# A graph network kernel: the second message layer in three sum passes with projections among them, and the degrees of its nodes summed in two places

## The reference

```python
def _priv_conv(h, src, dst, n, Wl, bl, Wr, scale):     # 128 -> 256, then 256 -> 128
    xn = _l2norm(h)
    agg = jax.ops.segment_sum(xn[src], dst, num_segments=n)   # with a loop edge for each node
    h_norm = jnp.linalg.norm(h, axis=-1, keepdims=True)
    out = _l2norm(agg) * h_norm * scale
    out = out @ Wl + bl + h @ Wr
    return _l2norm(out)
...
x = x + _L0_gnn_ref(h, ...)                            # two _priv_conv with a relu between them
h = jnp.maximum(_layernorm(x, axis=-1), 0.0)
...
def gcn_conv(x, W, b, src, dst, mask, n):
    h = x @ W
    deg = 1.0 + jax.ops.segment_sum(ew, dst, num_segments=n)
    dinv = jax.lax.rsqrt(deg)
    norm = dinv[src] * dinv[dst] * ew
    agg = jax.ops.segment_sum(h[src] * norm[:, None], dst, num_segments=n)
    agg = agg + h * (1.0 / deg)[:, None]
    return agg + b
```

## Time and profile before

| | us |
|---|---|
| median of 3 runs | 1125.64 (1122.07 to 1128.34) |
| the profiled execution, its own time | 1124.67 |
| its span on the core | 1122.5 |
| TensorE busy / VectorE busy / ScalarE busy | 936.8 / 572.8 / 396.0 |
| mean granted clock of TensorE | 0.918 |

### The profile page before, as it was taken

The page is one execution under the profiler, slowest core; times in us unless marked ns, Lnnn a source line. Parts: engine busy times, 40 slices in busy tenths (PEclk is TensorE's granted clock), DMA queues, the critical chain, the costliest instruction groups (busy, mean ns, idle before and its releaser), DMA issues.

```text
span 1122.5 us, 17876 instructions
## 1 busy us (share of the span) xinstructions
PE 936.8 (83%) x7347; PEld 608.7 (54%) x7347; DVE 572.8 (51%) x1630; ACT 396.0 (35%) x869; POOL 79.9 (7%) x102
## 2 busy tenths in 40 slices
PE   0346999998799999979999978988876785778997
PEld 0335666766555556965465545655535443454654
DVE  4799999986921011642120267545542654445222
ACT  1538999982661000372010031544104402220300
POOL 2100000000000000000000000741014100020000
PEclk9759999999899999859999999998988787889999
DMA  6430000007100000011000002774114200140002
GB/s 192 136 84 1 1 2 1 2 1 318 49 1 1 1 1 1 2 68 52 1 1 1 1 1 61 258 214 141 27 25 119 60 1 1 30 175 29 33 1 59
DMA packets 39794, 60.39 MB, mean 54 GB/s; under 512 B 3822, under 2 KB 30721, under 8 KB 39192
## 3 DMA queue, kind: packets, MB, share of 16 engines
q1 hardware_dynamic: 31202, 38.17, 10.3%
q0 software_dynamic: 4592, 17.86, 5.2%
q10 hardware_dynamic: 3910, 3.12, 1.1%
HBM read 33.08 MB, written 30.85 MB: 57 GB/s over the span
## 4 chain that ended last, share of the span: by engine, by line
PE 55%; DVE 32%; ACT 5%; DMA 4%; issue 3%; POOL 1%; ACTq 0%; DVEq 0%; POOLq 0%; SPq 0%
PE psum L2800 24%; PE psum L2260 12%; DVE region L1010 7%; DVE region L1003 6%; PE psum L2568 4%; PE psum L2165 2%; DVE region L1517 2%; PE psum L2762 2%; DMA half_table<-region 2%; PE psum L2344 1%; PE psum L2190 1%; DMA nodebuf<-in_x 1%; POOL region L778 1%; DVE region L1251 1%; PE psum L2782 1%
## 5 line engine op out<-in xcount | busy, mean ns | idle before, releaser
L2800 PE MATMUL psum<-adj,region 128*128 128x448 fp8e4 x1050 | 201.8, 353 | 0.0
L2800 PEld LDWEIGHTS psum<-adj,region 128*128 128x128 f16 x1050 | 102.5, 98 | 92.9
L2260 PE MATMUL psum<-adj,region 128*128 128x448 fp8e4 x700 | 135.5, 355 | 3.1 <-DVE region L1244 3.1
L2190 PE MATMUL psum<-region 128*128 128x200 bf16 (+2 forms) x1176 | 111.0, 229 | 20.6 <-DVE region L1010 20.5
L2190 PEld LDWEIGHTS psum<-region 128*128 128x128 bf16 x1176 | 93.2, 99 | 55.0 <-DVE region L1010 30.4
L2260 PEld LDWEIGHTS psum<-adj,region 128*128 128x128 f16 x700 | 68.7, 98 | 66.8 <-issue 5.2
L2800 PE MATMUL psum<-region 128*128 128x448 fp8e4 (+2 forms) x426 | 83.7, 359 | 13.6 <-DVE region L1710 13.5
L1862 ACT ACTIVATE adj<-psum 128x400 fp8e4<-128x400 f32 x196 | 86.7, 518 | 19.4 <-PE psum L2194 18.8
L1010 DVE TENSOR_TENSOR region<-iota_key,region 128x1200 bf16<-128x1200 bf16 x147 | 92.7, 703 | 0.0
L2165 PE MATMUL psum<-adj,region 128*128 128x448 fp8e4 x350 | 91.7, 355 | 0.0
L778 POOL DMA_INDIRECT region<-adj_table,node_of x33 | 31.2, 945 | 848.3 <-DVE node_of L1647 731.3
(11 more groups left out here) (348 smaller groups left out, 1209.0 us busy)
## 6 DMA issues: line engine op xcount, KB each, us to landing
adj_table<-adj SPq DMA_DIRECT2D x1, 10000.0 KB, 27.2
edge_table<-edges SPq DMA_DIRECT2D x1, 4656.0 KB
region<-dk_dram SPq DMA_DIRECT2D x2, 1568.0 KB, 8.3
adj_table<-region SPq DMA_DIRECT2D x1, 2704.0 KB, 8.9
half_table<-region SPq DMA_DIRECT2D x2, 832.0 KB, 7.1
node_table<-region SPq DMA_DIRECT2D x1, 1650.0 KB, 8.4
xs_dram<-nodebuf SPq DMA_DIRECT2D x1, 1600.0 KB, 6.1
nodebuf<-xs_dram SPq DMA_DIRECT2D x1, 1600.0 KB, 6.1
```

The source lines that it names most:

```text
L2190: pe.matmul(psum[:, q % BUILD_BANKS, i * KEYS + k0:i * KEYS + k1], hot_lo[:, r, c, j, :, i], hot_key[:, r, c, j, k0:k1, i], start=(n == 0) ...
L2260: last = pe.matmul(psum[:, b, 0:BLOCK], weight(t, k), adj[:, t * PAD + b * BLOCK:t * PAD + (b + 1) * BLOCK], start=(t == 0 and k == 0), st ...
L2800: last = pe.matmul(psum[:, b, 0:width], here[:, t, k, :], rows, start=(t == 0 and k == 0), stop=(t == n_src - 1 and k == 1))
```

## The change

The second layer's sums of m = 0 stay as they are. Those of m = 1 become three passes of 4, 2 and 1 blocks (AGG_PASSES). In the second pass TensorE makes seven projection groups and 14 norms between the products, in the third three groups and 6 norms, and behind it three groups and 5 norms. The copies out of PSUM of the second and third pass, and their squares, are ScalarE's. The rows are finished in three parts of 14, 6 and 5 tiles; the third one's add x, squares and scaled rows, and the transposes of groups 3 to 6, stand inside the first pass of the next convolution.

The degrees come from two places. Of the sources' tiles 0 to 9, one-column products in the first layer (250 products). Of tiles 10 to 24, VectorE adds the 128 lanes of `adj` (`sum_lanes`, 14 adds of 3136 columns into `lane_degrees`, f16, in `nodebuf`), and TensorE sums over the lanes (25 products) in the first pass, at tile 22. `early_degrees` (VectorE) and the degrees' transpose follow from there. Since `nodebuf` holds the lanes, x is loaded again only after the degrees. `packed_masks` is moved from `unet` to a place ahead of the adds.

```diff
@@ -514,11 +517,26 @@
...
-        EARLY = 4
-        LN_PARTS = ((0, 12), (12, TILES))
-        LN_LATE = 10
+        AGG_PASSES = ((0, 4), (4, 6), (6, BLOCKS))
+        LN_PARTS = ((0, 14), (14, 20), (20, TILES))
+        PROJECT_BANKS = (0, 1, 2, 3, 0, 1, 2, 3, 4, 5, 0, 1, 2)
+        PROJECT_FREED = (0, 0, 0, 0, 2, 4, 6, 8, 0, 0, 10, 12, 14)
+        PROJECT_AT = ({4: (0,), 6: (1,), 9: (2,), 11: (3,), 14: (4,), 16: (5,), 18: (6,)}, {9: (7,), 12: (8,), 15: (9,)})
+        NORMS_AT = (8, 18)
+        ROWS_FIRST = (2, 3, 1)
+        DEGREES_AT, TURN_DEGREES_AT = 22, 2
+        TURNED_FIRST = 3
+        TURN_BANKS_2 = (4, 5, 3, 7, 4, 5, 6)
+        TURNED_BEFORE = (1, 2, 3, 4, 5, 6, 7)
...
         ROW_PARTS = ((0, 8), (8, TILES))
         TURN_LAG = 8
+        COLUMN_TILES = 10
+        EARLY_COLUMNS = 13
+        EARLY_COL = 32
@@ -643,7 +661,6 @@
...
-            load_x(sp, x_again)
@@ -660,14 +677,15 @@
...
-                sp.wait_ge(centered, 3)
+                sp.wait_ge(deg_ready, 1)
+                load_x(sp, x_again)
+                sp.wait_ge(dkrows_ready, 1)
+                sp.dma_start(dk_dram[0], dk_rows_early).then_inc(dk_out, DMA)
+                sp.wait_ge(centered, 1 + len(LN_PARTS))
                 sp.dma_start(xs_dram[0], nodebuf[:]).then_inc(xs_out, DMA)
-                sp.wait_ge(dkrows_ready, 1)
...
-                sp.wait_ge(blocks_out, BLOCKS * FIRST_UNIT)
+                sp.wait_ge(squared, len(LN_PARTS))
                 sp.dma_start(d_all, row[0:1, 0:COLS].broadcast_to((P, COLS))).then_inc(db_in, DMA)
@@ -1140,14 +1159,41 @@
...
+            def sum_lanes():
+
+                lanes = lane_degrees[:, 0:COLS]
+                for t in range(COLUMN_TILES + 1, TILES):
+                    of = adj[:, COLUMN_TILES * PAD:COLUMN_TILES * PAD + COLS] if t == COLUMN_TILES + 1 else lanes
+                    step(nc.vector.tensor_tensor(lanes, of, adj[:, t * PAD:t * PAD + COLS], ALU.add))
+                nc.vector.memset(lane_degrees[:, COLS:PAD], 0.0).then_inc(lanes_summed, 1)
+
+            def early_degrees():
+
+                d, kept, deg = dcol[:, 0, 0, :], dcol[:, 0, 1, :], tiny[:, 10, :]
+                dve.wait_ge(deg_ready, 1)
+                step(nc.vector.tensor_copy(deg, psum[:, 7, EARLY_COL:EARLY_COL + TILES]))
+                step(nc.vector.tensor_tensor(deg, deg, psum[:, 7, 0:TILES], ALU.add))
+                step(nc.vector.tensor_scalar(deg, deg, 1.0 / COUNT, 1.0, ALU.mult, ALU.max))
+                rsqrt(d, deg, tiny[:, 11, :])
+                nc.vector.tensor_tensor(d, d, kept, ALU.mult).then_inc(dk_ready, 1)
+
             def second_layer(norm1):
...
+                blocks_of(1, 0, 4, first_agg(agg1t[:, 0, :]))
+                blocks_of(1, 4, BLOCKS, first_agg(agg1t[:, 0, :]))
+                early_degrees()
+
+                def take_blocks():
+
+                    dve.wait_ge(agg_half, 4 + 1)
+                    for b in range(*AGG_PASSES[0]):
+                        first_agg(agg1t[:, 1, :])(b).then_inc(blocks_out, 1)
+
...
                 dve.wait_ge(x_again, 2 * DMA)
+                take_blocks()
+                add_squares(0)
+                dve.wait_ge(dk_turned, 1)
+                v.tensor_copy(dk_rows_early, psum[0:2 * TILES, 7, P:2 * P]).then_inc(dkrows_ready, 1)
+                combine_part(0)
                 add_x(0)
-                combine(LN_PARTS[1][0] // 2, LN_LATE)
+                add_squares(1)
                 scale_rows(0)
-                combine(LN_LATE, len(GROUPS2))
+                combine_part(1)
+                add_squares(2)
                 add_x(1)
+                combine_part(2)
                 scale_rows(1)
+                return add_x, scale_rows
@@ -1302,16 +1383,15 @@
...
                     norm1 = first_layer()
+                    packed_masks()
+                    sum_lanes()
 
...
-                    second_layer(norm1)
-                    degrees(0, by_edges)
-                    dve.wait_ge(h2t_ready, len(GROUPS4))
-                    return
+                    return second_layer(norm1)
@@ -1705,6 +1778,10 @@
...
+                        if i == 0 and t == 4:
+                            add_x(2)
+                        if i == 0 and t == 8:
+                            scale_rows(2)
@@ -1956,26 +2032,39 @@
...
+                def take_blocks(n):
+
+                    act.wait_ge(agg_half, 4 + n + 1)
+                    for b in range(*AGG_PASSES[n]):
+                        act.wait_ge(squares_added, b - 2)
+                        nc.scalar.activation(new_squares[:, b % 3, :], psum[:, b, 0:BLOCK], ACT.Square, scale=1.0 / (UNIT_SCALE * COUNT)).then_inc(sq_ready, 1)
+                        nc.scalar.activation(agg1t[:, 1, b * BLOCK:(b + 1) * BLOCK], psum[:, b, 0:BLOCK], ACT.Copy,
+                                             scale=1.0 / (UNIT_SCALE * COUNT)).then_inc(blocks_out, 1)
...
+                def keep_turned(g):
+
+                    t0, n = GROUPS4[g]
+                    act.wait_ge(h2_turned, g + 1)
+                    nc.scalar.activation(nodes_t[:, t0 * P:(t0 + n) * P], psum[:, TURN_BANKS_2[g], 0:n * P], ACT.Copy).then_inc(h2t_ready, 1)
+
+                block_squares()
                 unit_squares(0)
+                take_blocks(1)
                 center_squares(0)
+                second_rows(0)
+                take_blocks(2)
                 unit_squares(1)
-                second_rows(0)
+                keep_turned(0)
                 center_squares(1)
+                keep_turned(1)
+                keep_turned(2)
                 second_rows(1)
-                for g, (t0, n) in enumerate(GROUPS4):
-                    act.wait_ge(h2_turned, g + 1)
-                    nc.scalar.activation(nodes_t[:, t0 * P:(t0 + n) * P], psum[:, g % 4, 0:n * P], ACT.Copy).then_inc(h2t_ready, 1)
@@ -2060,6 +2158,15 @@
...
+                        if i == 0 and t == 4:
+                            unit_squares(2)
+                        if i == 0 and t == 8:
+                            keep_turned(3)
+                            center_squares(2)
+                        if i == 0 and t == 12:
+                            second_rows(2)
+                        if i == 0 and t % 4 == 0 and t >= 16:
+                            keep_turned(t // 4)
@@ -2345,24 +2445,56 @@
...
-                pe.wait_ge(blocks_out, 2 * BLOCKS + 4)
-                for g in range(EARLY):
+                def part_norms(n):
+
+                    t0, t1 = LN_PARTS[n]
+                    pe.wait_ge(squares_added, AGG_PASSES[n][1])
+                    pe.wait_ge(dkrows_ready, 1)
+                    for t in range(t0, t1):
+                        last = pe.matmul(psum[:, NORMS_BANK[n], NORMS_COL + t:NORMS_COL + t + 1], agg_squares[:, t * P:(t + 1) * P], ones[:, 0:1],
+                                         start=True, stop=True)
+                    last.then_inc(norm_ready, 1)
+
+                def sum_degrees():
+
+                    pe.wait_ge(lanes_summed, 1)
+                    for t in range(TILES):
+                        last = pe.matmul(psum[:, 7, t:t + 1], lane_degrees[:, t * P:(t + 1) * P], ones_col[:], start=True, stop=True)
+                    last.then_inc(deg_ready, 1)
+
+                for n, (b0, b1) in enumerate(AGG_PASSES):
+                    pe.wait_ge(blocks_out, BLOCKS + (4 if n == 0 else BLOCKS))
+                    for t in range(TILES):
+                        if n == 0 and t == DEGREES_AT:
+                            sum_degrees()
+                        if n == 1 and t == TURN_DEGREES_AT:
+                            turn_degrees(0)
+                        if n > 0 and t == NORMS_AT[n - 1]:
+                            part_norms(n - 1)
+                        for g in PROJECT_AT[n - 1].get(t, ()) if n > 0 else ():
+                            pe.wait_ge(blocks_out, 2 * BLOCKS + AGG_PASSES[n - 1][1])
+                            project_tiles(g)
+                        for k in range(2):
+                            for b in range(b0, b1):
+                                last = pe.matmul(psum[:, b, 0:BLOCK], parts1[:, t, k, P:2 * P], adj[:, t * PAD + b * BLOCK:t * PAD + (b + 1) * BLOCK],
+                                                 start=(t == 0 and k == 0), stop=(t == TILES - 1 and k == 1))
+                    last.then_inc(agg_half, 1)
+                pe.wait_ge(blocks_out, 3 * BLOCKS)
+                for g in range(LN_PARTS[2][0] // 2, len(GROUPS2)):
+                    if g == LN_PARTS[2][0] // 2 + 1:
+                        part_norms(2)
                     project_tiles(g)
-                pe.wait_ge(squares_added, BLOCKS)
...
-                degree_sums(0, False)
-                pe.wait_ge(proj_done, 2 * TILES)
...
-                turn_degrees(0)
+                pe.wait_ge(proj_done, TILES + LN_PARTS[1][1])
+                for g in range(TURNED_FIRST):
+                    turn_second(g)
+
@@ -2376,11 +2508,20 @@
...
```

(21 more changed lines are left out.)

159 lines of the change are left out of this document (82 added, 77 removed).

## The result

| | kernel before | changed kernel |
|---|---|---|
| median of 8 runs | 1122.57 us (1118.39 to 1128.34) | 1135.67 us (1128.37 to 1139.51) |
| profiled execution | 1124.67 us, span 1122.5 | 1135.8 us, span 1133.9 |
| ratio, with its 95% interval | | 1.0107 (1.0079 to 1.0135) |

The changed kernel is 1.1% slower: the forecast's side, and 2.7 us above its 1133. That distance flatters the forecast. It added 8.5 us to 1124.67, and the median of the kernel before, over eight runs, is 1122.57; the ratio makes the difference 12.0 us (8.9 to 15.2). In the profiled pair it is 11.4 us of span.

What follows compares the result with a forecast made beforehand. TensorE's sums, then ScalarE and VectorE's row work, were taken to bound 343 to 547 us. Next convolution 2.1 us later, plus 1.6, 1.2 and 3.6 inside it, made 8.5 on 1124.67: forecast 1133 us, range 1115 to 1139.

Steps and rivals of the forecast that it cites:

- Column products at nothing: First layer: 250 degree products moved there fit into TensorE's gaps to within 0.2 us each; cost taken as 0.
- Adds at 3.45 us, end 388.0: VectorE, ahead of the bank copies: fourteen adds at one element at a time, 48.3 us from 339.7.
- Stall 16.5: Before the first pass: TensorE waits 16.5 us, from 374.4 to 390.9, for bank copies behind the adds.
- Clock behind the stall 1.6: First pass: TensorE's clock falls in the stall, costing 1.6 us more.
- Clock in the second pass, 1.5 behind the 14 norms: TensorE's second pass: slow clock behind the 14 norms costs 1.5 us.
- x 8.5 us behind the degrees: Reload of x waits for the degrees at 426.6, lands at 435.1; first projection waits 3.0 us.
- The end of the seventh projection at 465.7: Second pass on TensorE: the seventh projection group ends at 465.7 us, and the row work starts from there.
- The row work of three parts: VectorE and ScalarE, from 465.7: three parts in place of two; next convolution's first sum product at 508.1, against 506.0 before.
- Inside the next convolution: Its first pass: transposes 1.6 us, group 3's copy wait 1.2, group 4's 3.6, with no gap there before.
- rival (c): TensorE's clock stays low: projections 3 us more, cold start of the next convolution 1.6, x load 1.5; 1139 us, 11%.
- Rival (b): Stall stays, rest shorter: x in 6 us (-2.5), clock holds behind norms (-1.5), group 4's copy in time (-3); 1127 us, 26%.
- Rival (a): VectorE's adds go two elements at a time, end at 365.3; the stall and its clock loss go; 1115 us, 17%.

Runs made afterwards that it cites:

- fifteen column tiles: Changed kernel with 15 source tiles counted by column products in place of 10, so nine VectorE adds in place of fourteen; ratio to the kernel before 0.9949.
- two-byte kernel: Changed kernel with thirteen of the fourteen adds reading f16 zeros in place of fp8 tiles; ratio to the kernel before 0.992 (one run).
- split kernel: Changed kernel with one add left in place, seven behind the copies of banks 0 to 3, six behind those of banks 4 to 6; ratio to before 0.9917.
- second trace: Trace of the changed kernel run again without any edit, in the second group; 1173.23 us, ratio to the kernel before 1.0111.
- first pair: The original runs of the kernel before and the changed kernel, chip not on record; 1122.57 and 1135.67 us, ratio 1.0107.
- second group: Follow-up kernels run on another chip than the first group, among them the unedited changed kernel: 1173.23 us, ratio to the kernel before 1.0111.
- few degrees: Kernel before with 25 of its 625 degree products, those of source tile 0 alone; ratio to the kernel before 1.0009.
- first group: Fifteen column tiles, split kernel, early degrees and two-byte adds, run on one chip; ratios to the kernel before 0.9949, 0.9917, 0.9878 and 0.992.
- early degrees: Split kernel with the 25 products that sum the degrees at tile 15 of the first pass in place of 22; ratio to the kernel before 0.9878.
- copy first: Early degrees kernel with ScalarE's copy of turned group 4 ahead of part three's rows in place of behind them; ratio to the kernel before 0.9852.

## Why the prediction was right, point by point

- Column products at nothing: right, to 0.2 us. Beyond 250 they cost some 28 ns each (3.5 us for 125), as the fifteen column tiles show.
- Adds at 3.45 us, end 388.0: 3.43 with 3.46 from start to start, end 388.5. Right, and the reason (one operand of one byte) is shown by the two-byte kernel.
- Stall 16.5: 16.6. That it passes on in full is shown by the split kernel.
- Clock behind the stall 1.6: 2.15, and 1.84 in the second trace. I took it from the 3.06 us gap, behind which 56 products lost 1.6 us.
- Clock in the second pass, 1.5 behind the 14 norms: mis-sized. From the first projection group (438.70) to the end of the seventh it took 29.5 us for 28.3 forecast, 3.4 of them slow clock: 1.7 behind the norms, near the forecast, and 1.8 at the first projection group and the products behind it, right after the wait for x, for which I had nothing.
- x 8.5 us behind the degrees: 9.0 (the degrees' products end 427.4, VectorE goes on 436.4). The first projection waited 3.55 for 3.0.
- The end of the seventh projection at 465.7: 468.2, the sum of the points above. The error went through to the next convolution (508.1 forecast, 510.1 measured).
- The row work of three parts: 42.4 forecast, 41.8 measured. Its sum is right, its path is not quite: I led the middle of it over VectorE's factors and combining. In the trace it goes over ScalarE, by part one's 14 rows (485.59 to 491.1), the copy of block 6 behind them and part two's squares, to 493.7, and VectorE waits 1.1 us for these. By the prediction's numbers the two ways are level (both have part two's x added at 495.4), so this cost nothing here.
- Inside the next convolution I had 6.4 us more than before; measured 5.8 (9.9 - 4.1). That this is close is luck, since its parts were off: group 3's wait of 1.2 never came, group 4's was 2.1 for 3.6, and the transposes took 1.0 for 1.6, since those of group 3 stood ahead of the first sum product. In their place came a cold start of 2.5 us, which stood only in rival (c): 3.17 us for eight sum products that took 1.69 before (505.98), 1.91 for a group of 1.05, and 0.2 behind it.
- The end of the pass before was set at 546.9. It is 549.9 (537.83 + 12.08 in the fence above), so all my absolute times for that pass are 3 us low. The sum used differences and was not touched.
- Rival (b)'s 1127 adds its 1.5 us to the median, where the forecast and the other two rivals add theirs to the profiled execution; by that it is 1126.

Forecast 8.5, measured 9.9 by the mark, 11.4 by the span and 12.0 by the ratio. By the mark the errors are +2.0 up to the next convolution (2.5 of slow clock, less 0.6 in the row work) and -0.6 inside it. So the mechanism held (adds ahead of the copies, stall, three row parts), and the term most in error was TensorE's clock: 3.1 us in the sum, 5.6 in the two passes and 2.5 in the next convolution. Rival (a) fell by the adds. Rival (b) had two of its three terms wrong (x took 9.0 us, the clock did fall) and the third partly right (group 4's wait). Rival (c)'s cold start and projections at half speed were both seen, but for shorter stretches than it said. What stays open is the 1.5 us behind the mark.

## What to carry to other kernels

Work that an idle engine takes over is free only at a place where nobody's release stands behind it: list what the engine would have done next and who waits for that, and cut long work around it. Here thirteen of fourteen adds, placed behind the two sets of copies in place of ahead of them, turned 1.1% slower into 0.8% faster. Before work is moved off an engine, leave it out of the kernel once: if the time stays, as with the degrees, it lay beside something else. And a chain can be shortened only by the slack of what runs beside it: with about 1 us of it, a step moved forward by 3.8 us gave 0.9. Last, before a gain is credited to an edit, take the pieces that ran at another clock out of it.

## What the runs showed of the hardware

**An fp8 source.** A VectorE add of 3136 columns to f16 takes 3.42 us with one or two fp8 sources and 1.79 with f16 ones.

**The same kernel in two places.** The changed kernel took 1135.7 us in the first pair and 1173.2 in the second group, and the traces differ by 2.2 us at the mark. The other 35 us arise while the adjacency rows are gathered: the last cast of them stands at 887.8 us and at 927.1. Of them, 23.7 (27.7 + 9.1 - 13.1) are at the start of it, at VectorE's first casts of the gathered rows, here in the first pair and then in the second group:

```profile
723.82 16.42 DVE L1597 CAST region<-psum 128x512 fp8e4<-128x512 f32 x28 [13.09 <-PE psum L2776]
```

```profile
742.29 0.69 DVE L1597 CAST region<-psum 128x512 fp8e4<-128x512 f32 x1 [27.68 <-remote]
752.11 3.79 DVE L1597 CAST region<-psum 128x512 fp8e4<-128x512 f32 x6 [9.13 <-remote]
```

In the first pair they wait 13.1 us, in the second group 27.7 and then 9.1. The GpSimd instructions that start these gathers take 0.94 us each in both. It is not this kernel's doing: the kernel before waits 13.4 us there in the first pair, the one with few degrees 30.3 and 6.4 in the second group, and the split kernel 25.3 and 11.2 on the chip of the first group. The traces don't say why; the median from issue to landing of the gathers at L797 is 4.1 us in the first pair and 7.5 in the changed kernel's second trace, but 4.2 in the split kernel, which waits as long.

**The clock behind one-column products.** The group that stands behind the 14 norms, 28 instructions of one column, takes 1.95 us at full clock. With the same instructions in the same order ahead of it, it took 3.00 and 3.62 us in the two traces of the changed kernel, 3.11 with fifteen column tiles, 3.37 with the early degrees and 3.19 with the copy first, but 1.95 in the split kernel and with the two-byte adds. So the 0.72 and 1.00 of granted clock in the two windows above don't show that it was the place of the norms, two tiles earlier, that kept the clock up. I had put a fixed price on it; it isn't one.
